# The softmax numerator written back into the PSUM bank of the attended values

## The chip, the cores and the metric

One core of a Trainium2 chip runs the whole kernel. The metric is device time in microseconds, the median of several executions. A core has a matrix engine (TensorE, PE in the profile), a vector engine (VectorE, DVE), a scalar engine (ScalarE, ACT), GpSimd (POOL) and a queue for transfers (SyncE, SP), each with its own list of instructions, held together by semaphores. Matmul results land in PSUM, eight banks of 512 float32 per partition; everything else lies in SBUF. VectorE and ScalarE reach both memories, GpSimd works in SBUF here.

## The reference

A decoder layer on x of 8 batches by 128 tokens by 256 features:

```python
x = x + attn(layernorm(x), Wq, Wk, Wv, Wo)           # 16 heads of 16, masked scores, softmax
x = x + xattn(ctx, ctx, layernorm(x), ssm_kernel, D)  # a long convolution, multiplied by the query
x = x + ffn(layernorm(x), gate, up, down)             # 256 -> 2048 -> 256, 4-bit weights, tanh-gelu

# attn: the mask multiplies the scores, so a masked key still has the score 0 in the softmax
scores = jnp.einsum('bthd,bshd->bhts', q, k) * jnp.tril(...)
attn = jax.nn.softmax(scores / T ** 0.5, axis=-1)
out = jnp.einsum('bhts,bshd->bthd', attn, v).reshape(B, T, H * Dh) @ Wo
```

Since a masked score is 0 and not minus infinity, each row of the softmax has two parts: the keys up to the diagonal, with their exponentials, and the keys behind it, which all have the same weight. The kernel computes both parts and adds them before it divides.

## The kernel before, in words

The program is written out by hand, one fixed list for each engine. It has four stretches. First x is loaded, normalised, transposed and multiplied into queries, keys and values. Then the convolution of the context (`convolve`, 16 heads) is mixed with the attention scores. Then, from about 65 to 120 us, comes a pipeline over the eight batches in which attention, output projection, the query of the cross part, the cross product and the third normalisation of different batches are interleaved. From about 123 us to the end the feed-forward network runs, as a long list of matmuls (`gate_and_up`, `down`).

For one batch `b` the attention ends in these steps:

- `key_scores(b, p)` and, on ScalarE, `probs(b, p)` make the exponentials PT, eight heads at a time.
- `attend(b, g)` on PE (four calls, g = 0 to 3) multiplies them by the values and a column of ones (vaug) into bank 4 + b % 2, heads on partitions. The call with g = 0 first waits until the bank's last user, batch b - 2, is done with it.
- `pv_out(b)` on ScalarE copies the bank to SBUF (pvs). `turn_values(b)` on PE transposes it back into the same bank, so that tokens lie on partitions: 16 heads, each 16 values and one sum, at a step of 32 elements. It also puts the sums over the keys behind the diagonal into bank 6.
- `normalise(b)` on VectorE has four instructions, each waiting for the one ahead of it through the semaphore s_och: tail = bank 6 times the weight em (L958), num = tail + the attended values (L962), rec = 1 / num's column of sums (L965), o_sb = num times rec (L967). Here tail, num, rec, em and o_sb are tiles in SBUF.
- `turn_heads(b)` on PE waits for o_sb, transposes it into bank 7 (L1430). `take_heads(b)` on ScalarE copies it (oT, L659), `project_out(b)` multiplies it by Wo and adds X (L1465, L1467), `take_out(b)` writes X (L665).

Banks 6 and 7 are handed from user to user with `take`: the next user on PE waits for the last reader of the one before. So `project_out(6)` on PE waits for `ffn_lo(2)` on VectorE (xTl, L1041), which reads bank 7 for the feed-forward network's input and stands directly behind `normalise(7)` in VectorE's list. VectorE's list there is: `normalise(6)`, `sum_slots(3, 1)`, `normalise(7)`, `ffn_lo(2)`, `stats_ffn(3)`, `stats_cross(5)`.

Beside these run, on GpSimd, `conv_products(b, lc)` (L422 and L425, the products for the cross part, SBUF to SBUF), `decode_scale` (L438), `max_pieces` (L409), and the small rows of the normalisations, `rstds` (L355, L357). On VectorE stand the row maxima `pair_max` (mx L942, ms L951), the sums of the cross part (R, L1008), the low halves of the decoded weights (L998) and the statistics (L863, L865).

Of the kernel before, what the change touches and what calls it, by code (L numbers as in the profile page):

```python
# [10 lines left out]
ALU = mybir.AluOpType  # L11
# [6 lines left out]
H = 16  # L18
DH = D // H
# [19 lines left out]
def build(nc, x_d, ctx_d, wqkv_d, wo_d, ker_d, skip_d, gu_scale_d, down_scale_d, codes_d, out_d):  # L39
# [4 lines left out]
    with ctx:  # L44
        def sb(name, shape, dt=F32):
            return ctx.enter_context(nc.sbuf_tensor(name, shape, dt))

        def sem(name):
            return ctx.enter_context(nc.semaphore(name))

        def view(ap, dims, offset=0):

            return bass.AP(ap.tensor, ap.offset + offset, [list(ap.ap[0])] + [list(d) for d in dims])
# [64 lines left out]
        tail = sb("tail", [P, H, DH + 1])  # L118
        num = sb("num", [P, H, DH + 1])
        minus = num[0:2, :, :].rearrange("p h d -> p (h d)").bitcast(F16)[:, 0:HALF]  # L120
        rec = sb("rec", [P, H])
        o_sb = sb("o_sb", [P, 2, D])
# [26 lines left out]
        bank = [psum[:, i, :] for i in range(8)]  # L149
# [37 lines left out]
        s_och = sem("s_och")  # L187
# [670 lines left out]
        def _(ve):  # L858
            v_ = nc.vector
# [94 lines left out]
            def normalise(b):  # L954

                ve.wait_ge(s_suf, b + 1)
                ve.wait_ge(s_em, b + 1)
                v_.tensor_tensor(tail[:, :, :], bank[6][:, 0:272].rearrange("p (h d) -> p h d", h=H),  # L958
                                 view(em[:, b % 4, :], [[1, H], [0, DH + 1]]), ALU.mult).then_inc(s_och, 1)
                ve.wait_ge(s_och, 4 * b + 1)  # L960
                ve.wait_ge(s_tok, b + 1)
                v_.tensor_tensor(num[:, :, :], tail[:, :, :], view(bank[4 + b % 2][:, :], [[32, H], [1, DH + 1]]),  # L962
                                 ALU.add).then_inc(s_och, 1)
                ve.wait_ge(s_och, 4 * b + 2)
                v_.reciprocal(rec[:, :], num[:, :, DH]).then_inc(s_och, 1)  # L965
                ve.wait_ge(s_och, 4 * b + 3)
                v_.tensor_tensor(o_sb[:, b % 2, :].rearrange("p (h d) -> p h d", h=H), num[:, :, 0:DH],  # L967
                                 view(rec[:, :], [[1, H], [0, DH]]), ALU.mult).then_inc(s_och, 1)

            def codes_split(j):  # L970
# [129 lines left out]
            pair_max(3, 1)  # L1100
            pair_max(4, 0)
            normalise(0)
            pair_max(4, 1)
            pair_max(5, 0)
            w_lo(1)
            stats_cross(0)
            normalise(1)
            decode_codes(2)
            pair_max(5, 1)
            stats_cross(1)  # L1110
            normalise(2)
            pair_max(6, 0)
            sum_slots(0, 0)
# [84 lines left out]
        def _(pe):  # L1198
# [144 lines left out]
            def attend(b, g):  # L1343

                n = 4 * b + g
                pe.wait_ge(s_exp, n // 2 + 1)
                if g == 0:
                    if b == 0:
                        pe.wait_ge(s_vs, B)
                        pe.wait_ge(s_const, 7)  # L1350
                    if b >= 2:
                        pe.wait_ge(s_och, 4 * (b - 2) + 2)
                for j in range(4):
                    last = mmul(bank[4 + b % 2][32 * j:32 * j + DH + 1, P * g:P * g + P], vaug[:, b, 4 * g + j, :],
                                PT[:, n % PR, j, :], start=True, stop=True)
                last.then_inc(s_pv, 1)
# [159 lines left out]
            convolve(13, 1)  # L1516
            convolve(14, 0)
            attend(0, 0)
            attend(0, 1)
            attend(0, 2)  # L1520
            attend(0, 3)
            convolve(14, 1)
# [177 lines left out]
```

## Time and profile before

| | us |
|---|---|
| median of 3 runs | 256.91 (255.53 to 257.26) |
| the profiled execution's own time | 256.27 |
| its span in the profile | 254.5 |
| TensorE busy | 237.1 |
| VectorE busy | 159.0 |
| GpSimd busy | 135.5 |
| ScalarE busy | 126.9 |

The span is what the profiler saw, from the first to the last instruction. The time has 1.8 us more around it. A row of a timeline names the start, the duration, the engine and line, the operation, what is written from what, and in square brackets how long the engine had been idle and what ended that. [...]

### The profile page before, as it was taken

To read this page: it belongs to the slowest core of one execution; us is meant where nothing else is said; L and a number is where in the kernel's file an instruction comes from. 1 tells how busy PE (TensorE), PEld (TensorE's weight loads), DVE (VectorE), ACT (ScalarE), POOL (GpSimd) and SP (SyncE) were. 2 spreads that over 40 slices of the span, in tenths; PEclk is the share of its full clock that TensorE was granted. 3 is DMA by queue.
4 is the path that set the end of the run, shared out by engine and by line. 5 is a ranking of instruction groups with operands and counts; after the bars stand their busy time and mean duration, and the time that the engine had idled before them with its cause. 6 is when DMAs were issued, how large, how long until landed. Compare 5 with 4: busy or idle time off the path is not lost.

```text
span 254.5 us, 5449 instructions
## 1 busy us (share of the span) xinstructions
PE 237.1 (93%) x2100; PEld 149.1 (59%) x2100; DVE 159.0 (62%) x287; ACT 126.9 (50%) x273; POOL 135.5 (53%) x160
## 2 busy tenths in 40 slices
PE   7999999999999898857899999999999999999993
PEld 7755766556555455544445676656656566566562
DVE  2889647698899999796699975318244172322124
ACT  3355675577686886843776263334342433513230
POOL 4265164632229979796889931363544636333230
PEclk9999999999999999997999999999999999999999
DMA  6996996951121204000030000003030000000004
GB/s 180 371 341 178 178 234 207 151 105 61 39 92 30 101 3 123 9 0 0 3 124 0 0 3 0 3 2 124 3 114 11 0 3 0 0 3 0 0 3 165
DMA packets 15106, 18.85 MB, mean 74 GB/s; under 512 B 1448, under 2 KB 12776, under 8 KB 15080
## 3 DMA queue, kind: packets, MB, share of 16 engines
q1 hardware_dynamic: 15080, 18.49, 26.6%
q8 instruction: 17, 0.28, 0.4%
q14 instruction: 9, 0.07, 0.1%
HBM read 15.21 MB, written 3.15 MB: 72 GB/s over the span
## 4 chain that ended last, share of the span: by engine, by line
PE 76%; DVE 9%; POOL 4%; ACT 4%; issue 3%; DMA 2%; SPq 0%; DVEq 0%; ACTq 0%; POOLq 0%
PE bank L1227 39%; PE bank L1396 16%; PE bank L1283 4%; PE bank L1285 3%; PE bank L1281 3%; PE bank L1467 2%; DMA X<-in_x 2%; PE bank L1307 2%; DVE mx L942 1%; PE bank L1465 1%; POOL arena L422 1%; ACT PT L598 1%; DVE tail L958 1%; DVE o_sb L967 1%; DVE XN L1193 1%
## 5 line engine op out<-in xcount | busy, mean ns | idle before, releaser
L1016 DVE SCALAR_TENSOR_TENSOR QK<-bank,QK 128x512 f32<-128x512 f32 x32 | 21.9, 688 | 60.7 <-PE bank L1227 59.7
L446 POOL TENSOR_TENSOR QK<-QK 128x512 f16<-128x512 f32 x24 | 27.8, 1157 | 56.4 <-ACT QK L627 56.4
L637 ACT ACTIVATE QK<-bank 128x512 f32<-128x512 f32 x32 | 19.0, 595 | 60.9 <-PE bank L1227 60.8
L1227 PE MATMUL bank<-xTh,Wa 128*128 128x512 f16 x128 | 40.5, 379 | 0.6 <-DVE xTl L1041 0.6
L1227 PE MATMUL bank<-xTh,Wb 128*128 128x512 f16 x128 | 40.7, 379 | 0.0
L422 POOL TENSOR_TENSOR arena<-Ys,qx 128x640 f32<-128x640 f32 x16 | 25.4, 1591 | 4.1 <-ACT qx L680 4.1
L1227 PE MATMUL bank<-xTl,Wb 128*128 128x512 f16 x64 | 24.3, 379 | 0.0
L1227 PE MATMUL bank<-xTl,Wa 128*128 128x512 f16 x64 | 24.3, 379 | 0.0
L1396 PE MATMUL bank<-Wa,QK 128*128 128x256 f16 x192 | 23.6, 273 | 0.0
L942 DVE TENSOR_REDUCE mx<-bank 128x8 f32<-128x1024 f32 x16 | 19.5, 1219 | 6.2 <-PE bank L1315 6.1
L1396 PE MATMUL bank<-Wb,QK 128*128 128x256 f16 x192 | 23.3, 273 | 0.0
L1396 PEld LDWEIGHTS bank<-Wa,QK 128*128 128x128 f16 x192 | 18.8, 98 | 5.1
L1396 PEld LDWEIGHTS bank<-Wb,QK 128*128 128x128 f16 x192 | 18.7, 98 | 4.8
L627 ACT ACTIVATE QK<-QK 128x512 f16<-128x512 f32 x32 | 19.9, 623 | 2.2 <-DVE QK L1016 1.4
L1227 PEld LDWEIGHTS bank<-xTh,Wa 128*128 128x128 f16 x128 | 12.5, 98 | 14.3 <-issue 0.9
L383 POOL TENSOR_TENSOR arena<-arena 128x320 f32<-128x320 f32 x16 | 13.8, 875 | 13.3 <-PE bank L1285 13.3
L1227 PEld LDWEIGHTS bank<-xTh,Wb 128*128 128x128 f16 x128 | 12.5, 98 | 13.4
L355 POOL TENSOR_TENSOR rstd<-veps,nhalf 128x1 f32<-128x1 f32 x16 | 12.2, 760 | 13.6 <-ACT veps L643 13.6
L569 ACT ACTIVATE Ys<-bank 128x320 f32<-128x320 f32 x32 | 14.5, 455 | 9.5 <-PE bank L1285 8.0
L1008 DVE TENSOR_REDUCE R<-arena 128x128 f32<-128x1024 f32 x16 | 19.1, 1206 | 0.1
L438 POOL TENSOR_TENSOR w<-arena 128x768 f32<-128x768 fp8e4 x12 | 18.7, 1558 | 0.0
L598 ACT ACTIVATE PT<-bank 128x1024 f32<-128x1024 f32 x16 | 16.3, 1022 | 2.5 <-PE bank L1315 2.1
(129 smaller groups left out, 461.9 us busy)
## 6 DMA issues: line engine op xcount, KB each, us to landing
arena<-in_codes SPq DMA_DIRECT2D x6, 384.0 KB
arena<-in_ker SPq DMA_DIRECT2D x2, 1024.0 KB, 12.7
QK<-qk_scratch SPq DMA_DIRECT2D x8, 256.0 KB, 5.9
arena<-in_ctx SPq DMA_DIRECT2D x2, 768.0 KB, 8.8
qk_scratch<-Wa SPq DMA_DIRECT2D x12, 128.0 KB, 2.9
arena<-in_gu_scale SPq DMA_DIRECT2D x6, 256.0 KB
QK<-qk_scratch SPq DMA_DIRECT2D x8, 128.0 KB, 5.9
out<-XN SPq DMA_DIRECT2D x4, 256.0 KB, 2.4
```

What stands on the lines that cost most here:

```text
L422: g_.tensor_tensor(view(Z[:, r], [[64, H], [1, NPAIR], [NSLOT, HD]], rows), view(Ys[:, 0, 0], [every, [DIAG, NPAIR], [1, HD]], convolved), ...
L438: g_.tensor_tensor(W32[:, nib, :], bits(j)[:, 192 * nib:192 * nib + 192].bitcast(F8), scales(j), ALU.mult).then_inc(s_w32, 1)
L446: g_.tensor_tensor(il[:, u % IR], val[:, u % VR], ih[:, u % IR], ALU.subtract).then_inc(s_il, 1)
L569: s_.activation(view(Ys[:, h, lc], [[YROW, B], [DIAG, NPAIR], [1, HD]]), conv_bank(h, lc)[:, 0:320].rearrange("p (b d m) -> p b d m", b=B, ...
L598: s_.activation(PT[:, 2 * (n % 2):2 * (n % 2) + 2].rearrange("p g h t -> p g (h t)"), psum[:, 2:4, :], ACT.Exp, scale=SCALE).then_inc(s_ex ...
L627: s_.activation(ih[:, u % IR], val[:, u % VR], ACT.Copy).then_inc(s_ih, 1)
L637: s_.activation(val[:, u % VR], bank[2 * (u % 2)][:, :], ACT.Gelu_apprx_tanh, scale=1.0 / W_GAIN).then_inc(s_gel, 1)
L942: v_.tensor_reduce(mx[:, b % 2, 8 * p:8 * p + 8], psum[:, 0:2, :].rearrange("p g (h t) -> p (g h) t", h=4), AX.X, ALU.max).then_inc(s_max, 1)
L1008: v_.tensor_reduce(R[:, b % 2, H * half:H * half + H], view(Z[:, b % 2], [[NSLOT, H * HD], [1, NSLOT]], 1024 * half), AX.X, ALU.add).then_ ...
L1016: v_.scalar_tensor_tensor(out=val[:, u % VR], in0=bank[2 * (u % 2) + 1][:, :], scalar=UP_SCALE, in1=val[:, u % VR], op0=ALU.mult, op1=ALU. ...
L1227: ins = mmul(out, a(c), w(c), start=(n == 0), stop=(n == 3 * len(chunks) - 1))
L1396: last = mmul(out, a[:, u % IR, t], w[j % RW][:, nib, 512:768], start=((j, nib) == (0, 0) and tt % 2 == 0 and n == 0), stop=((j, nib) == ( ...
```

## The change

The sum tail + attended values is no longer written to the SBUF tile num but over the attended values, in place, in bank 4 + b % 2. The reciprocal reads its column of sums from there, and the last multiplication its 16 by 16 head outputs. Because the bank is now read until the last instruction of `normalise`, `attend(b, 0)` waits for the fourth count of batch b - 2 and no longer for the second. The number and the order of the instructions of each engine stay as they are, and no transfer is added or taken away. The tile num stays allocated.

```diff
                 ve.wait_ge(s_och, 4 * b + 1)
                 ve.wait_ge(s_tok, b + 1)
-                v_.tensor_tensor(num[:, :, :], tail[:, :, :], view(bank[4 + b % 2][:, :], [[32, H], [1, DH + 1]]),
-                                 ALU.add).then_inc(s_och, 1)
+                attended = bank[4 + b % 2][:, :]
+                v_.tensor_tensor(view(attended, [[32, H], [1, DH + 1]]), tail[:, :, :],
+                                 view(attended, [[32, H], [1, DH + 1]]), ALU.add).then_inc(s_och, 1)
                 ve.wait_ge(s_och, 4 * b + 2)
-                v_.reciprocal(rec[:, :], num[:, :, DH]).then_inc(s_och, 1)
+                v_.reciprocal(rec[:, :], view(attended, [[32, H]], DH)).then_inc(s_och, 1)
                 ve.wait_ge(s_och, 4 * b + 3)
-                v_.tensor_tensor(o_sb[:, b % 2, :].rearrange("p (h d) -> p h d", h=H), num[:, :, 0:DH],
+                v_.tensor_tensor(o_sb[:, b % 2, :].rearrange("p (h d) -> p h d", h=H),
+                                 view(attended, [[32, H], [1, DH]]),
                                  view(rec[:, :], [[1, H], [0, DH]]), ALU.mult).then_inc(s_och, 1)
@@ attend(b, g), g == 0
                     if b >= 2:
-                        pe.wait_ge(s_och, 4 * (b - 2) + 2)
+                        pe.wait_ge(s_och, 4 * (b - 2) + 4)
```

## Rows read from the trace of the kernel before

**Rows 1.** The profile's page: busy time by engine, and the granted clock by slice.
```profile
PE 237.1 (93%) x2100; PEld 149.1 (59%) x2100; DVE 159.0 (62%) x287; ACT 126.9 (50%) x273; POOL 135.5 (53%) x160
PEclk9999999999999999997999999999999999999999
```
**Rows 2.** Windows: length, busy (instructions) of PE, PEld, DVE, ACT, POOL, then clock.
```profile
113.00:114.00 1.00, 0.00 (x0) 0.00 (x0) 1.00 (x1) 0.16 (x1) 1.00 (x1) 1.00 0.00 0
116.00:117.00 1.00, 1.00 (x4) 0.82 (x3) 0.32 (x2) 0.16 (x1) 0.66 (x2) 0.50 0.00 0
123.00:250.00 127.00, 127.00 (x788) 77.28 (x787) 61.66 (x95) 50.77 (x87) 63.95 (x55) 1.00 0.06 20
```
**Rows 3.** The chain that ended last, in order of time: start, us, what.
```profile
88.16 0.44 DVE o_sb L967
...
101.41 0.61 ACT XN L651
...
112.81 1.68 DVE o_sb L967
...
117.84 0.39 ACT X L665
...
119.28 0.67 PE bank L1465 x2
...
120.85 0.39 ACT X L665
```
**Rows 4.** Instructions by line: minimum, median and maximum duration in ns.
```profile
L962 DVE TENSOR_TENSOR num<-tail,bank x8: 436/436/439, 65.8 to 112.0; 128x272 f32<-128x272 f32 x8
L967 DVE TENSOR_TENSOR o_sb<-num,rec x8: 424/426/1683, 66.5 to 112.8; 128x256 f32<-128x256 f32 x8
L1029 DVE TENSOR_TENSOR X<-X,bank x8: 386/408/421, 88.5 to 148.3; 128x256 f32<-128x256 f32 x8
L355 POOL TENSOR_TENSOR rstd<-veps,nhalf x16: 543/559/2067, 72.6 to 149.8; 128x1 f32<-128x1 f32 x16
```
**Rows 5.** Timeline of GpSimd.
```profile
80.03 0.75 POOL L355 TENSOR_TENSOR rstd<-veps,nhalf 128x1 f32<-128x1 f32 x1
96.71 1.77 POOL L422 TENSOR_TENSOR arena<-Ys,qx 128x640 f32<-128x640 f32 x1
100.04 1.28 POOL L357 TENSOR_SCALAR shift<-mv,rstd 128x1 f32<-128x1 f32 x1
111.69 1.01 POOL L425 TENSOR_TENSOR arena<-Ys,qx 128x384 f32<-128x384 f32 x1
112.65 1.56 POOL L422 TENSOR_TENSOR arena<-Ys,qx 128x640 f32<-128x640 f32 x1
```
**Rows 6.** Timeline of VectorE.
```profile
83.78 1.59 DVE L951 TENSOR_SCALAR ms<-mx,guard 128x16 f32<-128x16 f32 x1
96.52 0.52 DVE L967 TENSOR_TENSOR o_sb<-num,rec 128x256 f32<-128x256 f32 x1
99.40 1.78 DVE L998 SCALAR_TENSOR_TENSOR Wb<-w,Wb 128x1536 f16<-128x1536 f32 x1
112.05 0.44 DVE L962 TENSOR_TENSOR num<-tail,bank 128x272 f32<-128x272 f32 x1
114.41 0.41 DVE L1041 TENSOR_TENSOR xTl<-bank,xTh 128x256 f16<-128x256 f32 x1
```
**Rows 7.** Timelines of ScalarE and PE.
```profile
112.78 0.38 ACT L687 ACTIVATE xTh<-bank 128x256 f16<-128x256 f32 x1 [0.60 <-PE bank L1475]
97.04 0.63 PE L1354 MATMUL bank<-PT,vaug 128*17 128x128 f32 x16
98.41 0.44 PE L1430 MATMUL bank<-ident,o_sb 128*128 128x128 f32 x2 [0.74 <-DVE xTl L1041]
114.88 1.22 PE L1465 MATMUL bank<-X,ident 128*128 128x256 f32 x2 [2.13 <-DVE xTl L1041]
```
**Rows 8.** Groups by line of VectorE: count, then busy us, mean ns.
```profile
L898 DVE TENSOR_TENSOR Wa<-bank,Wa 128x512 f16<-128x512 f32 x6 | 4.0, 681 | 0.0
```

## The prediction, made before the changed kernel had run

> **What bounds the kernel now.** I read the busy times first, then the clock, then the chain, then the timelines around the one line that the change touches. PE is busy 93% of the span and its clock is full in all slices but one [rows 1]. From 123 to 250 us PE is busy for 127 of 127 us [rows 2]. So an earlier start of the feed-forward network is kept to the end, and all that the change can win or lose lies ahead of 123 us. There the order is set by handing work from engine to engine: the chain goes through the last instruction of `normalise` in batch 3 and in batch 7 [rows 3], and through batches 1 and 2 in the same way. Batch 7 is the odd one. Its o_sb takes 1.68 us, against a median of 0.426 for the eight [rows 3, 4].
>
> **Why that one is long.** GpSimd started a product of 1.56 us at 112.65, and o_sb, due at 112.81, ended at 114.49, just behind the end of that product at 114.21 [rows 3, 5]. It reads two SBUF tiles, num and rec. The num instruction of the same batch ran from 112.05 to 112.49 wholly inside another GpSimd product (111.69 to 112.70) and took its usual 0.44 us [rows 5, 6]; it reads one SBUF tile and one bank, and none of the eight exceeded 0.439 [rows 4]. The same conflict shows from the other side: the GpSimd product at 96.71 takes 1.77 instead of 1.56 beside o_sb of batch 4, the small L355 at 80.03 takes 0.75 beside o_sb of batch 2 where its median is 0.56, and L357 at 100.04 takes 1.28 under the two-tile instruction L998 [rows 4 to 6]. I read this as one path into SBUF that VectorE needs for a second SBUF input and shares with GpSimd. After the change o_sb reads one bank and one SBUF tile, the kind that was never held.
>
> **The change, part by part.**
>
> *o_sb of batch 7, no longer held.* From 1.683 to about 0.41 us. The next link, xTl L1041, also waits for ScalarE's xTh, which ends at 112.78 + 0.38 = 113.16 [rows 7], so it starts near 113.20 and not at 114.41 [rows 6]. On the path: -1.21 us. PE would then idle 0.92 us there instead of 2.13 [rows 7].
>
> *The clock behind it.* [...] From PE's start to ScalarE's start this step takes 117.84 - 114.88 = 2.96 us, and the same step of batch 7 at full clock 120.85 - 119.28 = 1.57 [rows 3]. So the fall costs 1.39 us. It came after an idle time of 2.13 us; the next longest one of PE in this stretch is 0.74 [rows 7], at 98.41, and no fall followed it. With 0.92 us the new idle time is nearer to that one, so I take the fall as gone: -1.39 us. Ends: 0 to -1.39.
>
> *Holds further up.* Without o_sb of batch 2 beside it, L355 at 80.03 is 0.20 shorter. GpSimd works without a break from there to 85.3, and the ms instruction at 83.78 is held (1.59 us) until GpSimd's work ends [rows 5, 6], so VectorE gets this 0.20 too, ahead of batch 3 on the chain. At 96.71 GpSimd gains 0.21, and VectorE 0.10 from a shorter o_sb in batch 4 (0.52 there). But L357 at 100.04 ends only when L998 lets go, and L998 gains only VectorE's 0.10; the chain goes on from it to XN at 101.41 [rows 3]. Sum: 0.20 + 0.10 = -0.30 us, if the chain between them keeps its gaps. Ends: 0 to -0.4.
>
> *The write into PSUM.* No VectorE instruction of this trace writes a bank, so the cost of num (0.436 us) is bounded. Above: if each element's write had to wait for a turn at the bank that is being read, it would take a second turn for each of 272 elements. A turn is (681 - 408) / 256 = 1.07 ns, from the same kind of instruction with 512 and 256 elements [rows 4, 8]. That is +0.29 us. Below, from the reads: with the bank in place of one SBUF input 256 elements take 0.408 instead of 0.426 [rows 4], -0.02. I take 0 for num, being nearest to these reads. For o_sb I take -0.02. The reciprocal's 16 elements are worth no more than a few turns either way, 0. Num counts on the path in batches 1, 2, 3, 4 and 7, five times: ends -0.1 to +1.45.
>
> [...]
>
> *The later release of the bank.* `attend(b, 0)` now waits for o_sb of batch b - 2. For b = 2 to 5 PE's own list has `turn_heads(b - 2)`, which waits for the same count, ahead of it. For b = 7, o_sb of batch 5 has long ended (by over 1 us) when PE gets to attend. For b = 6 it is close: attend starts at 97.04, o_sb of batch 4 ended at 96.52 + 0.52 = 97.04 too [rows 6, 7], and unheld ends at 96.93. I take 0.1 to 0.15 us for the signal to reach PE, so attend may start up to 0.05 later. Behind it in PE's list stand `attend(6, 1)` and `turn_heads(4)`, which is idle 0.74 us anyway for bank 7 [rows 7]. So 0; if that cover were gone, 0.05 to 0.2 us.
>
> **The sum.** -1.21 - 1.39 - 0.30 + 0 = -2.90 us. Against the profiled execution's 256.27 that is 253.4. The profile's time lies 0.64 below the median of the three runs, and I don't know which of them it resembles, so I add half of that: **253.7 us**, 1.2% under 256.91.
>
> **The rivals.**
>
> *A, the clock still falls* (20%). For it: PE has only handed-over work from 112.7 to 120 us, with several gaps of about 0.5, and an idle time of 0.92 is longer than any that the clock is known to survive here. Then 1.39 us of the gain is missing, or is paid a little later: 256.27 - 1.51 = 254.8, up to 255.4 by the median; within 1%.
>
> *B, PSUM is slower to write or read in place* (12%). By the upper bound 5 x 0.29 = 1.45 us come back: 254.8 to 255.5. For it: reads and writes of one instruction meet in one bank, which nothing in the trace does. Against it: reading a bank costs nothing extra here [rows 4]. [...]
>
> *C, slower than before* (7%). The same mechanism, but each element waits for more than one turn. The gain of 2.90 is used up at 2.90 / 5 = 0.58 us per num, two extra turns per element. At four, num takes 0.44 + 4 x 0.29 = 1.6 us, and the kernel 256.27 - 2.90 + 5.8 = 259.2. It would be the only such instruction here, since none reads and writes one bank. Nothing in the trace speaks for a cost of this size.
>
> *D, the change doesn't do what I read into it* (10%). If o_sb of batch 7 is held by its write into SBUF and not by its second input, it stays at 1.68 and only small terms are left: 256.0 to 256.9. Against it: num writes SBUF as well and was never held.
>
> *E, more is won* (4%): holds elsewhere also disappear because everything starts earlier, 252.0 to 252.8.
>
> **The numbers.** The forecast has 47%, its own range 252.8 to 254.6. With A and B that is 79%; the range needs a little of D and runs from 252.8 to 256.2. A change under 1%, 2.6 us, can't be told from none here. Faster by over 1% means below 254.3: nearly all of the forecast, E and a little of B, 50%. Within 1%: A, most of B, D and the upper edge of the forecast, 42%. Slower by over 1%, C and what I haven't seen, 8%.
>
> **What the changed profile would show.** The longest o_sb falls from 1.68 to about 0.41, whatever GpSimd does beside it. PE's idle time ahead of `project_out(6)` falls from 2.13 to about 0.9, the clock stays full in that slice, and the first matmul of the feed-forward network starts near 120.0 instead of 122.93. Num stays at 0.44; 0.72 would be B, over 1.0 C. The GpSimd rows that stood beside o_sb in batches 2 and 4 lose 0.2 each. An o_sb of 1.6 us would prove D, a clock of 0.50 near 115 with o_sb short A. What would make it wrong without any of these: another held instruction, such as ms, that meets GpSimd later and at a worse moment.

## The result and the profile after

The changed kernel takes 253.72 us (median of 6 runs, 253.43 to 254.18); the kernel before, run beside it, 257.09 (6 runs, 255.53 to 258.72). The ratio is 0.9885, with a 95% interval of 0.9842 to 0.9927. The profiled execution of the change took 253.43 us, its span is 251.7. One later execution of the kernel before took 405.23 us at a mean granted clock of 0.559; it is left out below.

The page of the changed kernel, busy times and granted clock. The slice that read 7 in [rows 1] is full now, and PE's busy time is 1.1 us less for the same matmuls. The 8 in the last slice is the clock behind the last matmuls: they end at 247.32, and the clock is 1.00 up to 249 and 0.50 from 250 us on. The second fence shows windows, in the form of [rows 2], from ahead of `project_out(6)` to the feed-forward network.
```profile
PE 236.0 (94%) x2100; PEld 149.2 (59%) x2100; DVE 157.7 (63%) x287; ACT 127.0 (50%) x273; POOL 134.7 (54%) x160
PEclk9999999999999999999999999999999999999998
```
```profile
113.00:114.00 1.00, 0.59 (x3) 0.54 (x4) 0.96 (x3) 0.00 (x0) 1.00 (x2) 1.00 0.00 0
114.00:116.00 2.00, 1.41 (x7) 0.72 (x5) 1.36 (x7) 0.94 (x4) 1.90 (x4) 1.00 0.00 0
116.00:123.00 7.00, 5.36 (x25) 3.12 (x26) 4.85 (x11) 4.65 (x10) 6.08 (x8) 1.00 0.00 0
```
The instructions of `normalise` by line (minimum, median, maximum in ns), against [rows 4]. L963 is the sum, now into the bank, L968 the last multiplication. The sum costs 446 ns instead of 436, o_sb 424 instead of 426, and the maximum of o_sb is 425 where it was 1683. The reciprocal, L966, went from 253 to 257.
```profile
L963 DVE TENSOR_TENSOR bank<-tail,bank x8: 445/446/447, 65.8 to 111.8; 128x272 f32<-128x272 f32 x8
L966 DVE RECIPROCAL rec<-bank x8: 256/257/259, 66.3 to 112.3; 128x16 f32<-128x16 f32 x8
L968 DVE TENSOR_TENSOR o_sb<-bank,rec x8: 424/424/425, 66.6 to 112.5; 128x256 f32<-128x256 f32 x8
```
The chain that ended last, around batch 7, as in [rows 3]. From PE's start of `project_out(6)` at 113.41 to ScalarE's at 115.00 are 1.59 us, against 2.96 before.
```profile
112.55 0.42 DVE o_sb L968
112.97 0.39 DVE xTl L1043
113.36 0.04 issue
113.41 0.70 PE bank L1467 x2
114.11 0.88 PE bank L1469 x4
114.98 0.02 issue
115.00 0.39 ACT X L665
```
The timeline of GpSimd. The product at 112.28 runs through o_sb of batch 7 (112.55 to 112.97) and neither waits. The two rows that stood beside o_sb in batches 2 and 4 went from 0.75 to 0.57 and from 1.77 to 1.58 [rows 5]. L357, which takes 0.27 us unheld, is still held (1.34 us), by the two-tile instruction of VectorE from 99.16 to 100.91.
```profile
80.05 0.57 POOL L355 TENSOR_TENSOR rstd<-veps,nhalf 128x1 f32<-128x1 f32 x1
96.56 1.58 POOL L422 TENSOR_TENSOR arena<-Ys,qx 128x640 f32<-128x640 f32 x1
99.70 1.34 POOL L357 TENSOR_SCALAR shift<-mv,rstd 128x1 f32<-128x1 f32 x1
112.28 1.56 POOL L422 TENSOR_TENSOR arena<-Ys,qx 128x640 f32<-128x640 f32 x1
```
The timeline of VectorE: ms is held 0.20 us less than in [rows 6], since GpSimd is ahead by so much; and the two-tile instruction.
```profile
83.81 1.39 DVE L951 TENSOR_SCALAR ms<-mx,guard 128x16 f32<-128x16 f32 x1
99.16 1.75 DVE L1000 SCALAR_TENSOR_TENSOR Wb<-w,Wb 128x1536 f16<-128x1536 f32 x1
```
The timeline of PE, against [rows 7]. The idle time ahead of `project_out(6)` is 0.93 us where it was 2.13. The last row is the first matmul of the feed-forward network, at 120.09; before, it started at 122.93. The difference of 2.84 us is that of the profiled times, 256.27 - 253.43.
```profile
96.95 0.63 PE L1356 MATMUL bank<-PT,vaug 128*17 128x128 f32 x16
98.17 0.44 PE L1432 MATMUL bank<-ident,o_sb 128*128 128x128 f32 x2 [0.59 <-DVE xTl L1043]
113.41 0.70 PE L1467 MATMUL bank<-X,ident 128*128 128x256 f32 x2 [0.93 <-DVE xTl L1043]
120.09 0.38 PE L1229 MATMUL bank<-xTh,Wa 128*128 128x512 f16 x1 [0.65 <-DVE xTl L1043]
```

### The profile page after: what moved, and what is told of

It reads as the page before. It is cut to its first block, busy times and chain, and to the rows that moved or that the text cites. A ratio compares the mean times of both kernels' runs of the same rounds, so it can differ in the third digit from the quotient of the medians.

```text
span 251.7 us, 5449 instructions
## 1 busy us (share of the span) xinstructions
PE 236.0 (94%) x2100; PEld 149.2 (59%) x2100; DVE 157.7 (63%) x287; ACT 127.0 (50%) x273; POOL 134.7 (54%) x160
## 4 chain that ended last, share of the span: by engine, by line
PE 81%; DVE 11%; ACT 3%; issue 3%; POOL 0%; DVEq 0%; POOLq 0%; ACTq 0%
PE bank L1229 39%; PE bank L1398 16%; PE bank L1285 4%; PE bank L1287 3%; PE bank L1283 3%; PE bank L1208 3%; PE bank L1469 2%; DVE mx L942 2%; PE bank L1309 2%; DVE R L1010 2%; PE bank L1467 1%; DVE tail L958 1%; DVE bank L963 1%; ACT PT L598 1%; PE bank L1356 1%
## 5 line engine op out<-in xcount | busy, mean ns | idle before, releaser
L355 POOL TENSOR_TENSOR rstd<-veps,nhalf 128x1 f32<-128x1 f32 x16 | 11.9, 747 | 11.4 <-ACT veps L643 11.4
```

## The experiments

The kernel before was run beside each group, so its median differs a little from group to group (256.73, 257.30, 257.26); each kernel is compared with that of its own group.

**One SBUF input by another way: rec in the bank, num in SBUF.**
```diff
-                v_.reciprocal(rec[:, :], num[:, :, DH]).then_inc(s_och, 1)
+                v_.reciprocal(view(bank[4 + b % 2][:, :], [[32, H]], DH + 1), num[:, :, DH]).then_inc(s_och, 1)
...
-                                 view(rec[:, :], [[1, H], [0, DH]]), ALU.mult).then_inc(s_och, 1)
+                                 view(bank[4 + b % 2][:, :], [[32, H], [0, DH]], DH + 1), ALU.mult).then_inc(s_och, 1)
...
-                        pe.wait_ge(s_och, 4 * (b - 2) + 2)
+                        pe.wait_ge(s_och, 4 * (b - 2) + 4)
```


> Num stays in SBUF as in the kernel before; instead the reciprocal is written into the attended bank, into the free column behind each head's sum, and o_sb reads num from SBUF and rec from the bank. So o_sb has one SBUF input, but another one than in the change. The bank is released at the fourth count, as in the change. Theory 1 (o_sb is held by GpSimd only when it reads two SBUF tiles): no o_sb above 0.45 us, PE's idle time ahead of project_out(6) 0.9 us, no fall of the clock, 253.7 us as the change. Theory 2 (the gain comes from num being in PSUM, by a cheaper write or read of it): o_sb of batch 7 stays near 1.7 us and the time near 257.

Measured: 253.77 us (253.29 to 254.03), ratio 0.9865 (0.9826 to 0.9905), as the change. Its o_sb by line, the GpSimd product that ran through o_sb of batch 7, and PE's start of `project_out(6)`:
```profile
L967 DVE TENSOR_TENSOR o_sb<-num,bank x8: 420/421/422, 67.0 to 113.0; 128x256 f32<-128x256 f32 x8
112.72 1.57 POOL L422 TENSOR_TENSOR arena<-Ys,qx 128x640 f32<-128x640 f32 x1
113.86 0.70 PE L1465 MATMUL bank<-X,ident 128*128 128x256 f32 x2 [0.93 <-DVE xTl L1041]
```
What counts is that one of o_sb's two inputs leaves SBUF. It doesn't matter which one: with the large one of 256 elements in the bank o_sb of batch 7 took 0.424 us beside the running product, with the one of 16, read sixteen times over, 0.42. Theory 2 falls: num itself was never the point.

**The change without batch 7, and in batch 7 alone.** In the first kernel the branch `b < 7` takes the changed lines and batch 7 the old ones; in the second only `b == 7` takes the changed lines, and the bank is released as before.
```diff
+                if b < 7:          # second kernel: if b == 7:
+                    attended = bank[4 + b % 2][:, :]
...
+                else:
+                    v_.tensor_tensor(num[:, :, :], tail[:, :, :], view(bank[4 + b % 2][:, :], [[32, H], [1, DH + 1]]),
+                                     ALU.add).then_inc(s_och, 1)
```


> The change in batches 0 to 6; batch 7 as before, with num in SBUF. Theory 1: o_sb of batch 7 meets the GpSimd product again and takes about 1.6 us, PE idles 2.1 us, the clock falls to 0.50 and project_out(6) takes 2.96 us; only the 0.3 us from further up is won, so 256.0 by the profiled execution and 256.8 by the median of 257.1. Rival (the gain is spread over the eight batches): about seven eighths of the gain are kept, 254.1.

> Only batch 7 has the new form; batches 0 to 6 as before, and the bank is released at the second count. Theory 1: o_sb of batch 7 at 0.42 us, PE's idle time 0.9 us, full clock, 2.6 us won: 253.7 by the profiled execution, 254.0 to 254.5 by the median. The rows of GpSimd beside o_sb in batches 2 and 4 stay at 0.75 and 1.77 us. Rival (spread gain): 0.4 us won, 256.6.

Measured: 256.77 us without batch 7 (254.64 to 258.32, 12 runs; ratio 0.998, 0.9942 to 1.0019), and 253.93 with batch 7 alone (253.26 to 254.34; ratio 0.9873, 0.9836 to 0.991). So all that the medians can tell of the gain comes from one instruction of eight. The 0.3 us from further up, expected without batch 7, doesn't show in its median of 256.77 against 256.73; it shows in the profiles, as told in the next section. The kernel without batch 7: o_sb of batch 7 by line, PE's start of `project_out(6)`, and three windows (length, busy times of PE, PEld, DVE, ACT, POOL, granted clock):
```profile
L978 DVE TENSOR_TENSOR o_sb<-num,rec x1: 1577/1577/1577, 112.7 to 112.7; 128x256 f32<-128x256 f32 x1
114.67 0.70 PE L1476 MATMUL bank<-X,ident 128*128 128x256 f32 x2 [2.03 <-DVE xTl L1052]
115.00:116.00 1.00, 1.00 (x5) 0.90 (x4) 0.93 (x4) 0.29 (x1) 0.14 (x1) 0.81 0.00 0
117.00:118.00 1.00, 0.69 (x2) 0.29 (x2) 0.81 (x3) 0.40 (x3) 0.61 (x1) 0.50 0.00 0
120.00:121.00 1.00, 1.00 (x4) 0.52 (x2) 0.00 (x0) 0.00 (x0) 1.00 (x1) 0.50 0.00 0
```
The hold is back (1.58 us) and the idle time (2.03). The clock fell a little later than expected, in the middle of `project_out(6)`, and was still at 0.50 in `project_out(7)` at 120 us. So the step that was to take 2.96 us took 2.07, and the next one, from PE's 118.43 to ScalarE's 121.37, took 2.94. Where the fall lands is not the same in each execution: in this one `project_out(6)` has 0.81 from 115 to 116 us, in the profile before 0.50. The kernel with batch 7 alone, o_sb by line in both forms, GpSimd's product beside it, and PE:
```profile
L969 DVE TENSOR_TENSOR o_sb<-bank,rec x1: 424/424/424, 113.0 to 113.0; 128x256 f32<-128x256 f32 x1
L978 DVE TENSOR_TENSOR o_sb<-num,rec x7: 424/426/529, 66.6 to 109.8; 128x256 f32<-128x256 f32 x7
112.79 1.56 POOL L422 TENSOR_TENSOR arena<-Ys,qx 128x640 f32<-128x640 f32 x1
113.80 0.70 PE L1476 MATMUL bank<-X,ident 128*128 128x256 f32 x2 [0.93 <-DVE xTl L1052]
```

**The clock alone: PE kept busy in its idle time, the hold left in.**
```diff
             def project_out(b):
 
+                if b == 6:
+                    pe.wait_ge(s_max, 2 * B)
+                    for _ in range(8):
+                        mmul(bank[0][:, 0:P], ident[:, :], ident[:, :], start=True, stop=True)
                 take(7, s_x1, b + 1)
```


> The kernel before, with eight more matmuls of the identity with itself on PE (into bank 0, which nobody needs then) ahead of project_out(6), about 1.7 us of work in the 2.13 us that PE idles there. The hold of o_sb stays. Theory 1 with the clock as a term of its own: the granted clock stays 1.00, project_out(6) takes 1.57 us from PE's start to ScalarE's instead of 2.96, the time falls by 1.4 us: 254.9 by the profiled execution, 255.7 by the median. Rival (the clock falls for another reason than PE's idle time): 256.3 to 257.1 as before, or more by what the fillers delay.

Measured: 255.11 us (254.77 to 256.41, 9 runs), ratio 0.9933 (0.9901 to 0.9965). Its o_sb by line, and PE with what is left of its idle time:
```profile
L967 DVE TENSOR_TENSOR o_sb<-num,rec x8: 424/426/1698, 66.7 to 113.0; 128x256 f32<-128x256 f32 x8
115.07 0.70 PE L1469 MATMUL bank<-X,ident 128*128 128x256 f32 x2 [0.36 <-DVE xTl L1041]
```
The hold stays (1.70 us) and yet 1.6 us are won, with `project_out(6)` at full clock: 115.07 to 116.67 on ScalarE, 1.60 us. So the two terms are separable: 1.6 us by the clock, and from 255.11 to the 253.77 of the first experiment, which belongs to the same group, another 1.3 by the hold and the smaller terms. The kernel before says the same where its clock happens not to fall: its 11 executions with a mean granted clock of 1.00 have a median of 255.14 us.

**GpSimd's product moved away instead.**
```diff
             conv_products(4, 0)
-            conv_products(4, 1)
             rstd_ffn(3)
             rstd_cross(5)
             rstd_cross(6)
+            conv_products(4, 1)
```


> The kernel before; only GpSimd's list differs: conv_products(4, 1), the product that stood beside o_sb of batch 7, comes three steps later, behind the small rows of the normalisations. o_sb still reads two SBUF tiles. Theory 1 (GpSimd's running product is what holds o_sb): o_sb of batch 7 takes 0.43 us, PE idles 0.9 us, full clock, 253.9 to 254.3 us. Rival (o_sb of batch 7 is long by itself, or through something else): 1.7 us and about 256.9 as before. If the later product delays the decoding and the cross products of batches 4 and 5 too far, PE would show an idle time behind 120 us and the time would lie between.

Measured: 254.79 us (254.57 to 255.8, 10 runs), ratio 0.9924 (0.9889 to 0.9958); the gain is smaller than forecast. Its o_sb by line, GpSimd at 99 us and its next row behind 112.96, and PE ahead of `project_out(6)` and behind the start of the feed-forward network:
```profile
L967 DVE TENSOR_TENSOR o_sb<-num,rec x8: 424/425/512, 66.2 to 113.1; 128x256 f32<-128x256 f32 x8
99.03 2.17 POOL L355 TENSOR_TENSOR rstd<-veps,nhalf 128x1 f32<-128x1 f32 x1
115.29 0.55 POOL L355 TENSOR_TENSOR rstd<-veps,nhalf 128x1 f32<-128x1 f32 x1 [2.33 <-ACT veps L643]
113.93 0.70 PE L1465 MATMUL bank<-X,ident 128*128 128x256 f32 x2 [0.93 <-DVE xTl L1041]
132.18 0.41 PE L1445 MATMUL bank<-ident,XN 128*128 128x128 f32 x2 [0.61 <-ACT XN L651]
```
o_sb with its two SBUF inputs is short as soon as GpSimd doesn't run a product beside it (the 0.51 is batch 4, with one). That closes the question of who holds it. The price is the idle time of 0.61 us at 132 us, which the expectation had named: GpSimd's list has no room for a product that comes later. The profile loses another 0.6 us that is not the move's doing, since both lists are as before in that place. L355 at 99.03 starts 0.02 us ahead of VectorE's two-tile instruction and takes 2.17 us; before, it started 0.01 us ahead of it (99.39 and 99.40) and took 0.55. So from tail of batch 0 to tail of batch 7 this profile has 46.88 us, against 46.28 before. In how many executions that happens is not shown.

**The later release of the bank alone.**
```diff
-                        pe.wait_ge(s_och, 4 * (b - 2) + 2)
+                        pe.wait_ge(s_och, 4 * (b - 2) + 4)
```


> The kernel before, with only the bank's later release (attend waits for the fourth count). attend(6, 0) starts up to 0.2 us later than at 97.04 behind turn_ffn(0), and the idle time of 0.74 us ahead of turn_heads(4) takes it in: 256.9 us as before.

Measured: 257.14 us (255.26 to 259.26, 10 runs), ratio 0.9985 (0.9935 to 1.0034). PE around `attend(6, 0)` in this kernel:
```profile
96.97 0.51 PE L1475 MATMUL bank<-ident,XN 128*128 128x128 f32 x2
97.61 0.63 PE L1354 MATMUL bank<-PT,vaug 128*17 128x128 f32 x16
98.83 0.44 PE L1430 MATMUL bank<-ident,o_sb 128*128 128x128 f32 x2 [0.60 <-DVE xTl L1041]
```
Attend starts 0.64 us behind the start of the step ahead of it, where it was 0.49 before (96.55 to 97.04), and the idle time behind it shrinks from 0.74 to 0.60. The wait is real and is taken in whole by that idle time, in this profile. The interval doesn't exclude a cost of 0.3%; from tail of batch 0 to tail of batch 7 the profile has 46.30 us, against 46.28 before.

**Further on: the two holds that are left.** The changed kernel still has ms held at 83.8 and L357 at 99.7. One kernel makes ms by a reduction, one moves the two-tile instruction on VectorE to a place with idle time, one does both. In the first diff, the lines that fill the guard's column and the one that writes mx beside it are left out.
```diff
-MAX_GAIN = 8.0
+MAX_GAIN = 1.0
-        mx = sb("mx", [P, 2, H])
+        mx = sb("mx", [P, 2, H, 2])       # the second of each pair holds the guard
-                    v_.tensor_scalar(ms[:, b % 2], mx[:, b % 2], guard[:, 0:1], 1.0 / MAX_GAIN,
-                                     ALU.max, ALU.mult).then_inc(s_ms, 1)
+                    v_.tensor_reduce(ms[:, b % 2], mx[:, b % 2, :, :], AX.X, ALU.max).then_inc(s_ms, 1)
```
```diff
             sum_slots(2, 0)
-            w_lo(2)
             normalise(5)
...
             stats_cross(6)
+            w_lo(2)
             decode_codes(3)
```


> The changed kernel once more, on the chip of the next three, so that they can be compared with it: 253.7 us.

> The changed kernel, and ms (the row maximum against its guard, one SBUF input) made by a reduction over pairs instead of the tensor-scalar instruction; the factor 1/8 becomes 1. Theory: GpSimd's path is also taken by a tensor-scalar of float32 from SBUF to SBUF, but not by a reduction, as R and mx are never held. Then the ms at 83.8 us takes 0.2 instead of 1.39, the ms at 77.1 0.2 instead of 0.57. Of the 1.2 us that VectorE gains only what its next wait leaves counts: tail of batch 3 waits for PE until about 86.4, so -0.3 to -0.5 us, 253.3. Rival (held for its small size or by chance): ms stays at 1.2 to 1.4 and the time at 253.7.

> The changed kernel, and the two-tile instruction of 1.75 us that makes the low halves of weight block 2 (VectorE, L1000, at 99.16 us, under which GpSimd's shift at 99.70 waits 1.34 us) is moved in VectorE's list from before normalise(5) to before decode_codes(3), where VectorE has 0.5 and 1.7 us of idle time. Theory: VectorE is the chain from 95 to 101 us, so tail of batch 5 comes 1.7 us earlier and the shift 1.1; PE's next waits take part of it, -0.8 to -1.3 us, 252.4 to 252.9. Rival: the weights' decoding on GpSimd waits for it and pushes the cross products of batch 5, no gain, 253.7 or above.

> The last two edits together: the sum of both gains if they lie on one chain one behind the other, 252.0 to 252.6.

Measured: the change again 253.69 us (253.48 to 254.18), ms by a reduction 253.23 (252.99 to 253.43), the two-tile instruction later 253.10 (252.41 to 254.14), both 252.73 (252.37 to 252.96, ratio to the kernel before 0.9831, 0.9785 to 0.9876). Each is 6 runs. The last one beats both kernels of this study. VectorE with ms by a reduction, and the GpSimd instruction that ran through it:
```profile
83.97 0.19 DVE L955 TENSOR_REDUCE ms<-mx 128x16 f32<-128x32 f32 x1
83.79 1.56 POOL L442 TENSOR_TENSOR w<-arena 128x768 f32<-128x768 fp8e4 x1
86.64 0.44 DVE L961 TENSOR_TENSOR tail<-bank,em 128x272 f32<-128x272 f32 x1
```
Ms is never held in this form, and 0.46 us are won, as expected. The edit also takes away guard, a second thing that the old instruction read from SBUF, so it doesn't tell whether the kind of instruction or this input made it liable. With the two-tile instruction later, GpSimd and VectorE:
```profile
100.13 0.27 POOL L357 TENSOR_SCALAR shift<-mv,rstd 128x1 f32<-128x1 f32 x1
100.58 0.44 DVE L958 TENSOR_TENSOR tail<-bank,em 128x272 f32<-128x272 f32 x1 [0.91 <-PE bank L1458]
116.07 1.93 POOL L357 TENSOR_SCALAR shift<-mv,rstd 128x1 f32<-128x1 f32 x1
```
L357 is no longer held at 100, and the hold has moved to 116 us, where it costs nothing visible. But the gain is 0.59 us and not 0.8 to 1.3: tail of batch 5 now waits 0.91 us for PE's L1458, the sums over the keys behind the diagonal. My working had missed that wait, since it was hidden under the instruction that I moved. The ranges of this kernel and of the repeated change overlap, but their profiles confirm the gain: 45.35 us from tail of batch 0 to tail of batch 7, against 46.01. The two gains add up (0.46 + 0.59 against 0.96).

## Why the prediction was right

By its own steps, each against the changed profile:

- **o_sb of batch 7.** Forecast: 0.41 us beside a running product, the next link 1.21 us earlier, PE idle 0.92. Measured: 0.424, PE idle 0.93, so 1.20 of idle time gone. Four runs show the cause: it is short with either input in a bank while the product runs, short without GpSimd beside it, long again with the old form in batch 7, and the new form in batch 7 alone is enough. Rival D is out.
- **The clock.** Forecast -1.39 us, from the 2.96 us of `project_out(6)` before, where the granted clock was 0.50 in each slice from 115 to 118 us, and the 1.57 of `project_out(7)` at 1.00. Measured in the profile 2.96 - 1.59 = 1.37, and 1.6 by the medians of the kernel that only keeps PE busy. Rival A is out: the mean granted clock was 0.995 or more in each of the 12 runs of the change, and in both of its profiles the clock is 1.00 from 112 to 123 us; the first one's 0.996 comes from the end, behind the last matmuls.
- **Holds further up.** Forecast -0.30. Measured at tail of batch 7: 111.30 against 111.58, -0.28. All but this term is within what the change in batch 7 alone wins. The experiments bear it out when tail of batch 7 is counted from tail of batch 0: 46.28 to 46.30 us in four profiles with the old form in batches 0 to 6 (before, the later release, the busy PE, batch 7 alone; the one with the product moved has its L355 held and is left out), 45.97 to 46.01 in the four profiles with a new form there (the change twice, rec in the bank, the change without batch 7).
- **The write into PSUM.** Taken as 0, bounded by -0.02 and +0.29 per num. Measured +0.010, with +0.004 for the reciprocal and -0.002 for o_sb: 12 ns per batch. Writing into the bank that is being read costs next to nothing here, 445 to 447 ns in the seven profiles that do it, against 436 to 439 into num; B and C are out.
- **The later release.** Forecast up to 0.05 us, hidden. Measured 0.05 in the change (96.40, where the step ahead starts, to 96.95, against 96.55 to 97.04), with 0.59 us of idle time behind it. The signal from VectorE to PE, taken as 0.1 to 0.15 us, is 0.15 in this profile, from the end of o_sb at 96.80 to attend at 96.95. It is 0.15 too with rec in the bank (96.83 + 0.42 to 97.40), with the later release alone (96.95 + 0.51 to 97.61), and in the kernel before from o_sb of batch 3 to `turn_heads(3)`, which waits for it (88.16 + 0.42 to 88.73, the fence below). For b = 7 o_sb of batch 5 ended at 102.76 before and at 102.49 in the change, and PE starts `attend(7, 0)` at 104.37 and at 104.10, 1.61 us behind in both. For b = 2 to 5 `turn_heads(b - 2)`, which started at 67.42, 74.19, 81.34 and 88.73 before, stands ahead of `attend(b, 0)` in PE's list.
```profile
88.16 0.42 DVE L967 TENSOR_TENSOR o_sb<-num,rec 128x256 f32<-128x256 f32 x1
88.73 0.41 PE L1430 MATMUL bank<-ident,o_sb 128*128 128x128 f32 x2 [0.53 <-DVE o_sb L967]
```

The sum, -2.90, met -2.84, and the feed-forward network started at 120.09 where the forecast had "near 120.0". That two single executions could be subtracted so closely is luck in part: tail of batch 0 starts at 65.30 and 65.31 us in them, but anywhere from 64.95 to 65.78 in the other ten profiles. What was not in the working is how much the kernel before varies. Its 51 runs beside the experiments fall into groups by their mean granted clock: 11 at 1.00 with 254.9 to 256.1 us, 16 at 0.993 with 255.4 to 257.6, 15 at 0.986 or 0.987 with 256.8 to 258.8, 7 at 0.979 with 258.1 to 259.2, 2 at 0.973 with 259.7 and 260.0. So the fall of the clock costs nothing in one execution in five and up to some 3.5 us in most others, 4.7 in the two slowest (from the 255.1 of the first group), and the profiled execution was one of the cheaper ones. By the medians the change wins 3.4 us and not 2.84. The predicted median was right because the changed kernel has no such spread (0.75 us over 6 runs) and its profile is typical; the 0.3 us that I added for the median of before landed on it by luck. Why the fall comes in one execution and not in another with the same idle time stays open.

## What to carry to other kernels

An instruction of VectorE whose duration varies between its repeats, with nothing before it in the chain to blame, is worth a look at what GpSimd runs in that moment; the cure can be as small as moving one of two SBUF inputs into a bank that is at hand. Price such a stall with what it does to PE's clock behind it: here about half of the gain was that. And before moving a long instruction out of the way, look for what the next one waits for underneath it.

## What the runs showed of the hardware

- VectorE with two inputs in SBUF and GpSimd, working in SBUF, held each other in these profiles. The one that started second mostly waited for the other's instruction to be over: o_sb of batch 7 took 1.683 us instead of 0.426 and ended 0.28 us behind the end of the product, L357 with its one element took 1.34 instead of 0.27 and ended 0.13 behind the end of the two-tile instruction. The first one was mostly lengthened only a little (o_sb of batch 4, 0.43 to 0.52), but an L355 that started 0.02 us ahead was held in whole (0.55 to 2.17). An input of 16 elements, read by broadcast, counts as the second input: with it in the bank all eight o_sb took 0.420 to 0.422. With one input in PSUM, none was held in any profile: num 0.436 to 0.439 us, or 0.445 to 0.447 into the bank, tail 0.418 to 0.442, o_sb 0.420 to 0.425.
- A tensor-scalar of float32 from SBUF to SBUF was held too (ms, 0.234 to 1.387 us with 16 elements in the changed kernel), although it has one tensor input beside the one-element guard. A reduction in its place was not: 185 to 188 ns in all eight. The reciprocal, also with one SBUF input, was never held (252 to 255 ns, eight times in the kernel before).
- VectorE read and wrote one bank in the same instruction nearly as fast as it read the bank and wrote SBUF: 446 ns for 272 elements, against 436.
- PE idle for 2.03 to 2.14 us was followed by a granted clock of 0.50 in all three profiles that have this idle time and no filler matmuls. By the mean granted clock (0.993 or less) the fall came in 40 of 51 executions of the kernel before. With an idle time of 0.93 us in the profile it never came: 0.995 or more in all 52 executions of those kernels.
